# Second feed-forward of a macaron block: where ScalarE normalises the group three ahead

## The reference, cut to what matters

```python
x = x + 0.5 * _L0_ffn_ref(_layernorm(x), kernel, bias, a, b)      # the third step
x = x + 0.5 * _L1_ffn_ref(_layernorm(x), r1_w, r1_b, r2_w, ...)   # the fourth step
# inside the fourth, with xf the normalised tokens:
ri = concatenate([xf, mean, std, min, max, l2, share of |xf| < 1e-6])
h = gelu(ri @ r1_w.T + r1_b)
probs = softmax(h @ r2_w.T)          # 32 experts, the two best of a token are taken
```

## Time and profile before

| | us |
|---|---|
| median of 3 runs | 1788.64 (1785.24 to 1790.99) |
| the profiled execution | 1788.87 |
| its span | 1787.2 |
| PE busy | 1488.8 (83% of the span) |
| DVE busy | 977.1 (55%) |
| ACT busy | 728.9 (41%) |
| POOL busy | 564.3 (32%) |

### The profile page before, as it was taken

How to read it: one execution, slowest core, us unless ns; L and a number is a source line. 1 busy time by engine, 2 the same in 40 slices (tenths; PEclk the granted TensorE clock), 3 DMA queues, 4 the chain that set the end, 5 groups by cost and what they waited for, 6 DMA issues and landing times. The chain is left out here.

```text
span 1787.2 us, 27066 instructions
## 1 busy us (share of the span) xinstructions
PE 1488.8 (83%) x9512; PEld 1127.3 (63%) x9512; DVE 977.1 (55%) x2816; ACT 728.9 (41%) x1775; POOL 564.3 (32%) x467
## 2 busy tenths in 40 slices
PE   6899989999999678339999997489995459999994
PEld 5566544555554454229889997255553349899994
DVE  8865677787873597855531111356566855521110
ACT  5222147666667375415423232114333425322331
POOL 6522210000000442321636455221211231636535
PEclk9989889999999898559999999699997569999997
DMA  3034363333300022325969894401112326879974
GB/s 104 18 127 129 107 131 63 79 55 79 55 26 1 12 95 83 150 44 174 246 194 258 245 246 65 133 25 35 48 36 95 118 71 201 225 221 247 265 193 47
DMA packets 113493, 212.11 MB, mean 119 GB/s; under 512 B 20085, under 2 KB 79386, under 8 KB 104154
## 3 DMA queue, kind: packets, MB, share of 16 engines
q1 hardware_dynamic: 87066, 178.93, 31.8%
q0 software_dynamic: 26304, 31.60, 11.4%
HBM read 158.71 MB, written 51.38 MB: 118 GB/s over the span
## 5 line engine op out<-in xcount | busy, mean ns | idle before, releaser
L952 DVE TENSOR_REDUCE attnm_top<-psum 128x1 f32<-128x384 f32 (+3 forms) x384 | 212.8, 597 | 56.4 <-PE psum L1037 52.3
L1174 ACT ACTIVATE attnm_prob<-psum 128x512 f32<-128x512 f32 (+1 forms) x384 | 192.1, 530 | 87.6 <-PE psum L1047 81.0
L2328 POOL DMA_INDIRECT x_sum<-moe1e_y,moe_scatter_i x76 | 119.7, 1575 | 128.2 <-ACT moe1e_y L2462 71.0
L2507 DVE SCALAR_TENSOR_TENSOR moe1e_h<-moe1e_gate,psum 128x160 f32<-128x160 f32 x160 | 50.6, 321 | 199.4 <-ACT moe1e_gate L2436 199.1
L2328 POOL DMA_INDIRECT out<-moe2e_y,moe_scatter_i x76 | 119.2, 1568 | 127.7 <-ACT moe2e_y L2462 70.5
L2507 DVE SCALAR_TENSOR_TENSOR moe2e_h<-moe2e_gate,psum 128x160 f32<-128x160 f32 x160 | 50.4, 321 | 198.8 <-ACT moe2e_gate L2436 198.6
L2383 PE MATMUL psum<-moe1e_xgT,moe_w_up 128*128 128x160 f32 x1024 | 152.2, 304 | 2.4 <-ACT moe1e_xgT L2452 2.4
L2383 PE MATMUL psum<-moe2e_xgT,moe_w_up 128*128 128x160 f32 x1024 | 150.7, 302 | 2.4 <-ACT moe2e_xgT L2452 2.4
L2383 PEld LDWEIGHTS psum<-moe1e_xgT,moe_w_up 128*128 128x128 f32 x1024 | 144.2, 193 | 4.8 <-issue 4.8
L2383 PEld LDWEIGHTS psum<-moe2e_xgT,moe_w_up 128*128 128x128 f32 x1024 | 142.7, 192 | 4.8 <-issue 4.8
L1348 POOL DMA_INDIRECT moe_xg<-xn_rows,moe_gather_i x80 | 84.3, 1054 | 159.3 <-DVE moe_gather_i L1536 93.0
(11 more groups left out here) (414 smaller groups left out, 3230.5 us busy)
## 6 DMA issues: line engine op xcount, KB each, us to landing
moe_w_up<-in_expert_up SPq DMA_DIRECT2D x64, 1024.0 KB, 7.5
moe_w_down<-in_expert_down SPq DMA_DIRECT2D x64, 512.0 KB, 3.5
attnm_q_hat<-q_parts SPq DMA_DIRECT2D x72, 128.0 KB, 4.4
moe_a_up<-in_adapter_up SPq DMA_DIRECT2D x32, 256.0 KB, 4.2
q_parts<-attnf_q_part SPq DMA_DIRECT2D x12, 512.0 KB, 2.8
attnm_k_hat<-k_parts SPq DMA_DIRECT2D x72, 64.0 KB, 2.3
x_res<-in_x SPq DMA_DIRECT2D x8, 512.0 KB, 9.4
v_tails<-attnf_v_tail SPq DMA_DIRECT2D x4, 1024.0 KB, 4.3
```

Source lines behind the costliest of these rows:

```text
L952: nc.vector.tensor_reduce(top[:, n // QUADS % 2, tiles[0]:tiles[-1] + 1, hh:hh + 1], s.ps[:, u.bank, 0:len(tiles) * width].rearrange("p (t ...
L1174: nc.scalar.activation(prob[:, i % NPROB, at:GROUP], s.ps[:, u.bank, at:GROUP], ACT.Exp).then_inc(taken[u.bank], 1)
L2328: nc.gpsimd.indirect_dma_start(total, bass.IndirectOffsetOnAxis(ap=rows, axis=0), y[:, q, k, :], None, bounds_check=TOKENS + SPARE - 1, oo ...
L2507: nc.vector.scalar_tensor_tensor(out=h[:, n % 2, i, :], in0=gate[:, i, :], scalar=1.0 if i < INTER // P else SCALE_A, in1=s.ps[:, u.bank, ...
```

## The change

In each round of ACT, norm(i+3) moves from its place behind copy_x(i-1) to the place directly behind copy(i+2), ahead of abs, under and count of group i-1. Nothing is added or removed, and the other four engines' queues are untouched.

```diff
                 if 0 <= i + 2 < GROUPS:
                     copy(i + 2)
+                if 0 <= i + 3 < GROUPS:
+                    norm(i + 3)
                 if 0 <= i - 1 < GROUPS:
                     r.absolute(act, i - 1)
                     r.under(act, i - 1)
...
                 if 0 <= i - 1 < GROUPS:
                     r.copy_x(act, i - 1)
-                if 0 <= i + 3 < GROUPS:
-                    norm(i + 3)
                 if 0 <= i - 2 < GROUPS:
                     r.gelu(act, i - 2)
```

## The result

The changed kernel took 1796.39 us (median of 18 runs, 1790.05 to 1801.86), the kernel before 1789.65 us (18 runs, 1785.24 to 1791.63). The ratio is 1.0041, with an interval of 1.0030 to 1.0051. So the change costs 0.4%, some 7 us, where the forecast was 2 and its range ended at 1795.5.

What follows compares the result with a forecast made beforehand. The prediction took a ring of PE, copy, statistics passes and copy_s as the bound. Two norms gain 2.1 less 1.5 us, two cost 1.3 + 1.98; it took 2.0 later, 1790.9 (1790.6 against the median), range 1786.0 to 1795.5.

Steps and rivals of the forecast that it cites:

- The ring: In full rounds PE, copy, abs and statistics passes, copy_s and PE again wait on each other in turn, 10.65 us a round.
- The early gain: Rounds 1 and 2: norm(4) and norm(5) early bring a gain of 2.1 us at full clock.
- the slow clock in round 2: After 4.1 us idle before turn_s(0), PE runs some 3.3 us at half clock, costing about 1.5 of the 2.1.
- The unknown of 2 us for the reductions beside bias(4): Round 2: DVE's reductions might stall under bias(4), some 2 us; taken as nothing, left in the range.
- The waits before hidden(1) and hidden(2): Rounds 3 and 4: PE's waits grow from 0.67 and 0.96 us to about 2.0 and 2.9.
- Rival 2: DVE is the bound and bias adds leave its router norms in peace: gain of 8.2 us, 1780.5; chance 0.05.
- rivals 3 and 4: 3: early gain holds, 1 to 2 us earlier, 1787, chance 0.09; 4: nothing moves, 1788.6, chance 0.08.
- the sum: Four moved norms: two gain 2.1 us less 1.5 of slow clock, two cost 1.3 + 1.98; 2.0 later taken.
- fast end: The lag after round 4 if PE keeps its full clock: 0.5 us.
- the 0.6 for norm(6): Round 3: norm(6) costs 1.3 us, less perhaps 0.7 if PE keeps its clock and the table load is away.
- slow end: The lag after round 4 at the slow clock, from a loss of 0.5 in round 2: 3.1 us or somewhat more.
- rival 1: Longer waits before hidden(1) and hidden(2) let PE's clock fall: 5 to 7.2 us later in all, 1794.6; chance 0.16.

Runs made afterwards that it cites:

- last_one: The changed kernel with only norm(7) early and the other norms in their old place; 1797.03 us, ratio 1.0043 to the kernel before.
- first_two: The changed kernel with only norm(4) and norm(5) early, norm(6) and norm(7) in their old place; 1787.81 us, ratio 0.9987 to the kernel before.
- after_all: The changed kernel with filler transposes before turn_s(0), hidden(1), hidden(2) and in three tail gaps; 1786.84 us, ratio 0.9982 to the kernel before.
- before_all: The kernel before with filler transposes before turn(4) and in three tail gaps; 1786.97 us, ratio 0.9987 to the kernel before.
- small_bias: The kernel before with POOL's bias add on one feature of 256; 1789.24 us, ratio 1.0004 to the kernel before.
- half_one: The kernel before with only two of the four instructions of norm(7) early; 1793.81 us, ratio 1.0027.
- after_split: The changed kernel with copy_s between the second and third of count's four sums; 1790.97 us, ratio 1.0009 to the kernel before.
- after_again: The changed kernel run once more, unchanged; 1797.24 us (6 runs), ratio 1.0053 to the kernel before.
- last_two: The changed kernel with only norm(6) and norm(7) early; 1795.71 us, ratio 1.0046 to the kernel before.
- last_one_tail: last_one with filler transposes before turn_s(5), hidden(6) and hidden(7), none before hidden(2); 1792.89 us, ratio 1.0019 to the kernel before.
- combined: first_two with copy_s between count's second and third sum, copy_s(6) first in round 8, picks of groups 0 to 3 before finish(7); 1784.51 us, ratio 0.9975.
- combined_busy: combined with 24 filler transposes before turn_s(0) and turn_s(5), and 7 before hidden(7); 1778.77 us (6 runs), ratio 0.9940 to the kernel before.
- before_tail: The kernel before with filler transposes before turn_s(5), hidden(6) and hidden(7); 1786.67 us, ratio 0.9987 to the kernel before.

## Why the prediction was wrong

**Right, and shown.** The ring. In rounds 4 and 5 its 10.65 us stayed 10.55 to 10.66 wherever norm was out of it, the clock full and the counts not split, and one norm made it 12.61 (last_one). The early gain: first_two's stretch is 1.93 us shorter. By the full-clock kernels the two early norms lead by 1.98 us at turn(5) (26.62 us from turn(2) in after_all, 28.60 in before_all), where the prediction had 2.1, and the slow clock in round 2 took 1.4 of it (28.06 in after), where it had 1.5. turn(4) behind turn_x(0) with no wait; router norm(1) at 1.37 us; finish(0) held until bias(5) ended, 642.47 + 0.90 = 643.37 against 640.99 + 2.35 = 643.34. The unknown of 2 us for the reductions beside bias(4) is zero, at 1.22 and 1.21 us. The Trainium skill (VectorE: DVE Perf Modes, the perf-mode tier table) puts `tensor_reduce` in the 1x mode alone; with the GPSIMD Engine Reference as the prediction read it, it forecast this zero, and the trace agrees. The waits before hidden(1) and hidden(2) were forecast at about 2.0 and 2.9 us and came as 2.85 and 2.94, so the first was sized 0.85 too small. Rival 2 was refuted by small_bias, rivals 3 and 4 by the result.

**What the sum alone was worth.** With the clock kept, the difference is 0.5 us by the means (after_all against before_all), known to about 2.5, and 1.45 in the stretch of the two profiled executions (74.28 against 72.83), where the first two norms give 1.98 and the last two cost 3.43. The sum's fast end had 0.5, from 2.1 less 0.6 and 1.98; what it had too low is the 0.6 for norm(6), which is 1.46 from turn(5) to hidden(1) (8.70 against 7.24). With the slow clock of round 2, which the sum did price, the traces of before and after give 2.15, for the 2.0 that I took. So the sum of moved work was right. Its slow end was added up wrong: a loss of 0.5 with 1.3 and 1.98 makes 3.8 us and not 3.1, and as the range's end was put higher anyway, nothing hangs on it.

**The step that failed** is rival 1's price and its place outside the sum, the line "A fall costs the product of L1817 and what follows it 1.5 to 2.6 us, and two of them 3 to 5.2", with the chance of 0.16 behind it. Three things in it were wrong. First, it stood as a rival and not in the sum. The evidence taken against it, that waits up to 0.96 us never cost the clock, says nothing on waits of 2.9, and the only row with such a wait had the clock at half. The range ended at 1795.5, below the 1795.8 of rival 1's own upper end. Second, "it decides from an idle time of about 2.9 us" took a threshold from one row. The clock fell at 0.86 (before, hidden(7)), 1.94 (half_one) and 2.85 (after), and held behind 2.05 (after_split), 2.85 (after_again), 2.94 and 3.58 (after). The Trainium skill (TensorE: Matmul & The Clock Gate, its list of rules) asks for no idle gaps over about 3 us; all three falls lie below that, so here the rule isn't enough to be safe. Third, the price was taken from one slow product and what follows it. That was about right in three executions: a fall made its round 1.4 us longer in after and last_one and 1.7 in after_again. But the slow stretch ran 10 us in last_two and half_one and 12.4 us in last_one_tail, and the work in it lies on the ring: the round from hidden(2) to hidden(3) is 14.61 us in the first two and 15.94 in the third, 4.0 and 5.4 more than the ring's.

In numbers: the forecast of +2.0 should have been about +0.5 for the work, by the means, and about +7 for the clock. The chance of rival 1 should have been the larger one, and its time some 2 us later than I made it.

**What stays open.** In the profiled executions the stage is 2.9 us longer (after), while the medians are 6.7 apart. The 2.9 are 1.3 ahead of the first moved norm, 3.5 in the ring's stretch, and 2.4 given back in the tail, where the clock came back sooner behind turn_s(5) and held behind the 3.58 us: 23.61 us against 25.98. The remaining 0.4 lie between the last logits and the barrier. The spans differ by 5.7 us, and the rest of that is 1.5 ahead of the stage and 1.3 far behind it. From the end of this stage to the last rstd of the first expert layer nothing differs: it is 475.67 us before (719.40 to 1195.07) and 475.70 after (723.79 to 1199.49). So no single pair of traces locates the 7 us of the means. It is the filled kernels that tie them to the clock. The profiled execution of after is one of its faster ones, 1794.63 against a mean of 1796.53, and its clock fell once in the full rounds, for 3.2 us. In the 18 executions the time falls with the core's mean granted clock (1790.05 us at 0.912, 1801.86 at 0.905), which fits slow stretches of varying length, but none of the traces is of an execution as long as 1801.86. What in a program's history decides whether a given gap costs the clock was not found either.

## What to carry to other kernels

When work is moved between two waits of a ring, add up the moved microseconds, then look at which wait of TensorE grows, and price that wait as if the clock fell behind it, for as long as the slow stretches of the same kernel last. With one wait grown from 0.96 to 2.92 us the kernel was slower by more than three times the work that made it grow. To know how much of a difference is clock, fill all the gaps of both versions with harmless transposes and compare these; filling one gap alone leaves the clock free to fall at the others.

## What the runs showed of the hardware

- The fall isn't tied to one length of idle: 1.94 us was followed by 10 us at half clock, though PE was busy for all of them, and the clock fell at a wait of 0.86 us (before, hidden(7)). Behind 2.94 and 3.58 us it held (after). The same wait of the same program went either way in two executions.
- Transposes whose result nobody reads made kernels faster: 2.4 us in before_all (ratio 0.9975 to 0.9999) and 5.8 us from combined to combined_busy, whose intervals lie apart. The 2.2 us of before_tail are not clear of no change (0.9973 to 1.0002).
- GpSimd's bias add held up a small VectorE instruction to its end, a COPY of 128x8 for 0.90 us where it takes 0.16 to 0.17 alone, but not a reduction of 128x1024 beside it, 1.22 us either way.
